# Probabilities-times-values products of a local attention, issued in halves with a 128-row product between the halves

## The reference, cut to what matters

```python
x = _layernorm(x + L0_attn(x))     # linear attention
x = _layernorm(x + L0_xattn(x))    # 4 experts
x = _layernorm(x + L0_ffn(x))      # 8 gated experts, golden weights
x = _layernorm(x + L1_attn(x))     # local attention in groups of 32 tokens
x = _layernorm(x + L1_xattn(x))    # attention over ctx
x = _layernorm(x + L1_ffn(x))      # shared and routed experts, top 2
```

```python
scores = jnp.einsum('bhgqd,bhgkd->bhgqk', qg, kg) / np.sqrt(hd)
attn = jax.nn.softmax(jnp.where(causal, NEG, scores), axis=-1)
out = jnp.einsum('bhgqk,bhgkd->bhgqd', attn, vg)
```

## Time and profile before

| | |
|---|---|
| time, median of 3 runs | 430.19 us (429.94 to 431.14) |
| span of the profiled execution, first to last instruction | 429.5 us |
| TensorE, busy | 413.5 us (96%) |
| GpSimd, busy | 270.6 us (63%) |
| VectorE, busy | 255.2 us (59%) |
| ScalarE, busy | 241.6 us (56%) |
| mean granted TensorE clock | 0.997 |
| chain that ended last, PE's share | 75% |

### The profile page before, as it was taken

How to read it: one execution, slowest core, us unless ns; L and a number is a source line. 1 busy time by engine, 2 the same in 40 slices (tenths; PEclk the granted TensorE clock), 3 DMA queues, 4 the chain that set the end, 5 groups by cost and what they waited for, 6 DMA issues and landing times.

```text
span 429.5 us, 9350 instructions
## 1 busy us (share of the span) xinstructions
PE 413.5 (96%) x3645; PEld 361.4 (84%) x3645; DVE 255.2 (59%) x637; ACT 241.6 (56%) x423; POOL 270.6 (63%) x237
## 2 busy tenths in 40 slices
PE   8999999999999999899999999999699999999994
PEld 7888999988889888788888899798578989888983
DVE  4778657748536338966654588655455676343243
ACT  4848654764484775352734767573526757554543
POOL 1744454564798577674876548457647386877763
PEclk9999999999999999999999999999999999999998
DMA  8644000021233313042222103121523332565402
GB/s 256 195 149 145 3 2 0 2 76 50 73 91 123 103 53 124 24 127 96 79 86 76 38 0 111 51 88 63 167 74 96 118 103 78 151 165 151 141 33 98
DMA packets 19623, 39.29 MB, mean 91 GB/s; under 512 B 2763, under 2 KB 7371, under 8 KB 19580
## 3 DMA queue, kind: packets, MB, share of 16 engines
q1 hardware_dynamic: 19004, 38.17, 28.8%
q10 hardware_dynamic: 576, 0.53, 0.4%
HBM read 37.08 MB, written 1.08 MB: 89 GB/s over the span
## 4 chain that ended last, share of the span: by engine, by line
PE 75%; DVE 10%; issue 4%; ACT 4%; DMA 3%; SPq 2%; POOL 1%; POOLq 0%; DVEq 0%; ACTq 0%
PE bank L492 13%; PE bank L493 13%; PE bank L495 13%; PE bank L762 8%; PE bank L764 7%; PE bank L763 7%; PE bank L842 2%; DMA pk_raw<-w_attn_dram 2%; PE bank L781 2%; PE bank L830 1%; DVE q_buf L1584 1%; DMA brow<-cw_dram 1%; PE bank L515 1%; PE bank L812 1%; PE bank L813 1%
## 5 line engine op out<-in xcount | busy, mean ns | idle before, releaser
L1307 POOL TENSOR_TENSOR h_lo<-hraw,h_hi 128x512 fp32r<-128x512 f32 x76 | 98.1, 1294 | 77.3 <-ACT h_hi L1097 77.2
L492 PE MATMUL bank<-xT_hi,pk_hi 128*128 128x512 f32 x256 | 102.9, 402 | 1.1 <-DVE hraw L1625 1.1
L493 PE MATMUL bank<-xT_hi,pk_lo 128*128 128x512 f32 x256 | 101.0, 395 | 0.0
L1097 ACT ACTIVATE h_hi<-hraw 128x512 fp32r<-128x512 f32 x76 | 47.8, 629 | 72.3 <-DVE hraw L1625 70.3
L1625 DVE TENSOR_TENSOR hraw<-bank,sil 128x512 f32<-128x512 f32 x76 | 52.4, 689 | 54.6 <-ACT sil L1085 24.6
L495 PE MATMUL bank<-xT_lo,pk_hi 128*128 128x512 f32 x256 | 80.4, 395 | 0.0
L762 PE MATMUL bank<-pk_hi,h_hi 128*128 128x256 f32 x272 | 77.8, 286 | 0.2 <-issue 0.2
L764 PE MATMUL bank<-pk_hi,h_lo 128*128 128x256 f32 x272 | 76.9, 283 | 0.0
L763 PE MATMUL bank<-pk_lo,h_hi 128*128 128x256 f32 x272 | 76.8, 282 | 0.0
L1313 POOL TENSOR_TENSOR pk_lo<-pk_raw,pk_hi 128x512 fp32r<-128x512 f32 (+1 forms) x44 | 74.8, 1700 | 2.8 <-ACT pk_hi L1115 2.6
L492 PEld LDWEIGHTS bank<-xT_hi,pk_hi 128*128 128x128 f32 x256 | 48.2, 188 | 11.8 <-DVE hraw L1625 1.6
(11 more groups left out here) (256 smaller groups left out, 736.6 us busy)
## 6 DMA issues: line engine op xcount, KB each, us to landing
pk_raw<-pk_f_dram SPq DMA_DIRECT2D x28, 384.0 KB, 3.3
pk_raw<-pk_f_dram SPq DMA_DIRECT2D x16, 512.0 KB, 3.5
pk_raw<-pk_f_dram SPq DMA_DIRECT2D x16, 256.0 KB, 3.3
kv_buf<-pk_x_dram SPq DMA_DIRECT2D x4, 512.0 KB, 3.7
x_tok<-x_rows_dram SPq DMA_DIRECT2D x1, 1024.0 KB, 9.5
pk_raw<-pk_x_dram SPq DMA_DIRECT2D x4, 256.0 KB, 6.2
brow<-cw_dram SPq DMA_DIRECT2D x4, 256.0 KB, 3.4
cw_late<-cw_dram SPq DMA_DIRECT2D x4, 256.0 KB, 4.0
```

What stands on the lines that cost most here:

```text
L492: pe.matmul(o, w(kc)[0], x(kc)[0], start=kc == 0, stop=False)
L493: pe.matmul(o, w(kc)[1], x(kc)[0], start=False, stop=False)
L1097: A(h_hi[:, row, at * 512:(at + 1) * 512], hraw[:, s % 2, :], ACT.Copy).then_inc(sems["hid_hi"], 1)
L1307: pool.tensor_tensor(h_lo[:, row, q], hraw[:, s % 2, :], h_hi[:, row, q].bitcast(F32), ALU.subtract).then_inc(sems["hid_lo"], 1)
```

## The change

Each `a1_values(T)` becomes two calls of 32 program matmuls (64 MATMUL records and 64 weight loads each): heads 0 to 7 where the whole stood, and heads 8 to 15 in a new step one product later. `a0.40`, `a0.55`, `a0.41`, `a0.56` are the second halves of tiles 0, 1, 2 and 3, and `a1.40` to `a1.56` those of tiles 4 to 7. Only the second half tells DVE. First halves keep the waits; second halves have none. The lists of the other engines are as before.

```diff
-u38 g39 u39 d18 a0.10 g40 u40 a0.25 g41 u41 a0.11 d19 a0.26 g42 d20 u42 g43 u43 g44 e0.2 e1.2 u44 e0.3 e1.3 g45 u45
+u38 g39 u39 d18 a0.10 g40 a0.40 u40 a0.25 g41 a0.55 u41 a0.11 d19 a0.41 g42 a0.26 d20 a0.56 u42 g43 u43 g44 e0.2 e1.2
...
-            def a1_values(T):
-
-                for hd in range(HEADS):
+            def a1_values(T, part):
+
+                for hd in range(part * HEADS // 2, (part + 1) * HEADS // 2):
...
-                m.then_inc(sems["a1_o_ps"], 1)
+                if part:
+                    m.then_inc(sems["a1_o_ps"], 1)
...
+                elif i in (40, 55, 41, 56):
+                    a1_values(T0 + (40, 55, 41, 56).index(i), 1)
```

More of the change, by code:

```diff
@@ L139 @@
 g31 u31 d14 d15 g32 u32 g33 u33 g34 e0.12 e1.12 u34 g35 u35 a0.3 d16 a0.4 g36 u36 g37 a0.5 a0.6 u37 a0.7 g38 a0.8 d17
-u38 g39 u39 d18 a0.10 g40 u40 a0.25 g41 u41 a0.11 d19 a0.26 g42 d20 u42 g43 u43 g44 e0.2 e1.2 u44 e0.3 e1.3 g45 u45
[L141 to L145, removed]
+u38 g39 u39 d18 a0.10 g40 a0.40 u40 a0.25 g41 a0.55 u41 a0.11 d19 a0.41 g42 a0.26 d20 a0.56 u42 g43 u43 g44 e0.2 e1.2
+u44 e0.3 e1.3 g45 u45 g46 e0.4 e1.4 u46 e0.5 e1.5 d21 g47 u47 e0.7 e1.7 d22 a0.22 d23 g48 u48 g49 e2.12 e3.12 u49 g50
+a0.24 a1.3 a1.4 u50 d24 a1.5 a1.6 a1.7 g51 a1.8 u51 g52 u52 d25 d26 d27 a1.10 g53 a1.40 u53 a1.25 g54 a1.55 u54 a1.11
+g55 a1.41 u55 a1.26 d28 a1.56 d29 d30 d31 g56 u56 e2.2 e3.2 g57 e2.3 e3.3 u57 g58 u58 e2.4 e3.4 d32 d33 e2.5 e3.5 g59
+u59 g60 u60 d34 e2.7 e3.7 g61 u61 a1.22 d35 d36 g62 d37 u62 g63 a1.24 u63 g64 u64 g65 u65 d38 g66 d39 d40 d41 u66 g67
+u67 g68 u68 d42 g69 u69 g70 u70 g71 d43 d44 d45 u71 g72 d46 u72 g73 u73 g74 u74 g75 u75 d47 e48 e49 e50 f48 e51 f49
+f50 f51
 """.split()
@@ L926, in attention @@
                     pe.wait_ge(sems["a1_pT"], 2 * h + 1)
-                    a1_values(T0)
+                    a1_values(T0, 0)
                 elif i == 25:
-                    a1_values(T0 + 1)
+                    a1_values(T0 + 1, 0)
                 elif i == 11:
@@ L932, in attention @@
                     pe.wait_ge(sems["a1_o"], T0 + 1)
-                    a1_values(T0 + 2)
+                    a1_values(T0 + 2, 0)
                 elif i == 26:
                     pe.wait_ge(sems["a1_o"], T0 + 2)
-                    a1_values(T0 + 3)
+                    a1_values(T0 + 3, 0)
+                elif i in (40, 55, 41, 56):
+                    a1_values(T0 + (40, 55, 41, 56).index(i), 1)
                 elif i == 22:
```

## The result

| | before | after |
|---|---|---|
| time, median of 6 runs each on one chip | 430.12 us (429.55 to 431.14) | 433.26 us (432.63 to 434.49) |
| ratio after to before, 95% interval | | 1.006 (1.0039 to 1.0081) |
| span of the profiled execution | 429.5 us | 431.3 us |
| TensorE, busy | 413.5 us | 415.5 us |

The change is slower by 0.6%. Before's span plus the same 1.8 is 431.3, some 1.1 us above its median.

What follows compares the result with a forecast made beforehand. TensorE, busy 413.5 of 429.5 us, was taken to bound the kernel, idling at instruction-block ends. First half +2.4 us and second half 0, on the 430.19 median, gave 432.6, rounded to 432.5 us; range 430.1 to 434.2.

Steps and rivals of the forecast that it cites:

- The price of going in and out: On PE, each of eight more runs of small products costs 0.30 us, 2.4 us in all, 1.2 per half of the batch.
- Tile 3 and `e1.2`: Tile 3 ends later; its chain of 8.3 us against PE's 6.3 makes PE wait 2.0 us at e1.2's transposes.
- The sum of the first half: Tiles 0 to 3: +1.2 for entries, -0.8 for holes removed, +2.0 wait at e1.2, together +2.4 us.
- Tile 4's block is late "because of a transfer that began before the tile": Tile 4's instruction fetch waits for a weights' transfer, block there at 305.93 again; PE waits 1.05 us instead of 2.7.
- Tile 5's block "comes at 311.67 again": Tile 5's fetch falls into the weights' transfer of 306.0 to 309.3 as before; PE waits 1.35 us.
- second half: 0: Tiles 4 to 7: what splitting gains is given back at e3.2, whose chain PE waits for; 0 us net.
- Rival 1: The fetches of tiles 4 and 5 clear, tile 5 ends 1.3 to 2.3 us earlier: 430.2 to 431.2 us; chance 0.20.
- Faster: All 5.6 us of idle time go and neither chain makes PE wait: 427.0 us; chance 0.12.
- The holes stay: PE's holes at small products remain; entries, e1.2 and e3.2 cost 3.8 us: 434.0 us; chance 0.15.
- same: Whole-kernel time within 0.3% (1.3 us) of before, 428.9 to 431.5 us; chance 0.20.
- rival 3: PE's holes at small products stay, with 3.8 us added: 434.0 us; chance 0.15.

Runs made afterwards that it cites:

- Experiment 2: The change with tile 3 whole in its old place: 430.1 us, ratio 0.9994; with tile 3's halves one product earlier: 430.57 us, 1.001.
- experiment 1: Against the kernel before: only tiles 0 to 3 split, 434.51 us, ratio 1.0078; only tiles 4 to 7 split, 429.94 us, 0.9983; before run again, 431.66 us.
- experiment 4: The kernel before, with one weights' transfer on SP held until tile 4 has ended: 431.09 us, ratio 1.001.
- experiment 5: The kernel before, with tile 3's first 10, 2 or 64 products issued twice: 426.22, 430.45 and 435.4 us, ratios 0.9924, 1.0013 and 1.0131.
- the weights held back: The kernel before, with one weights' transfer on SP issued only when tile 4 is done: 431.09 us, ratio 1.001.
- 2 and 64 products twice: The kernel before, with the first 2, or all 64, products of tile 3 issued twice: 430.45 us (ratio 1.0013) and 435.4 us (1.0131).
- the second half alone: The kernel before with only tiles 4 to 7 in halves, tiles 0 to 3 whole: 429.94 us, ratio 0.9983.
- the shift of 10: Tile 3's first 10 products issued twice: on the kernel before 426.22 us, ratio 0.9924; with tiles 4 to 7 also split 428.26 us, 0.9989.

## Why the prediction was right, and where two of its steps were not

The number (432.5 forecast, 433.26 measured), the sign and the mechanism that carries it held. That the number came so near is in part luck: the first half cost 1.0 us more than forecast, the second gave 0.7 that was not, and part of what was said of tiles 4 and 5 had the wrong cause.

*The price of going in and out* is right: 0.10 us beside 64 x 0.0085 at a half, 0.11 at the next step (231.79 to 232.13, where it is 0.23), and 0.09 more from the last product ahead of a half to its first record, 0.30 as forecast.

*Tile 3 and `e1.2`* is right. From tile 3's end to the issue of R1 pass 0.87 us (231.79 to 232.66; forecast 0.88) and from there to the end of the norm 7.39 us (to 238.96 + 1.09; forecast 7.40). The wait is 1.62 us in the list and 1.8 between starts. The product behind the transposes comes 2.8 us after their first one (237.49 to 240.30) where it took 0.8 in before (236.07 to 236.86): 2.0, as forecast. Experiment 2 shows that the place of tile 3 carries the sign, with down 20's wait, which goes with it.

*The sum of the first half* was too small: +2.4 forecast, +3.2 in the profiles and +3.4 in experiment 1. What was left out is the wait of down 20, 0.7 us. The prediction followed the delay of tile 3 through DVE and said nothing of tile 2, though its own rule was that DVE hears of a tile only after the second half; behind `a1_out` of tile 2 stand the additions that down 20 waits for.

*Tile 4's block is late "because of a transfer that began before the tile"* is wrong (experiment 4). Its packet starts late also with idle DMA engines; that PE's sequencer, standing at tile 4's wait, asks for it late is my reading (experiment 5). The time at which it is there counts from tile 4's start, so the forecast came out near for another reason: PE goes on 3.76 us after that start in before, 3.38 in after, 3.21 with the weights held back, 3.48 and 3.54 with 2 and 64 products twice. The forecast hole of 1.05 us was 0.7 in after and 0.6 with the second half alone.

*Tile 5's block "comes at 311.67 again"* is wrong as well. Its packet started in after while the weights were moving, and PE went on 5.2 us after it had gone on in tile 4, not 5.7: a hole of 0.8 between starts, not 1.35. With that tile 5 ended 0.9 us sooner, seen from tile 4's start (8.9 us against 9.7). The chain through R2, C7 to C9 and R3 to `e3.2` followed it, and took 0.8 us less itself between tile 5's end and the product behind `brow` (314.68 to 322.40, 7.7 us, against 8.5), and 0.2 less from there (DVE's timeline of after):

```profile
322.40 0.69 DVE L1613 TENSOR_TENSOR sil<-bank,brow 128x512 f32<-128x512 f32 x1 [2.13 <-DMA brow<-cw_dram]
```

So the term "second half: 0", from the step that the gain of tiles 4 to 7 is given back at `e3.2`, was mis-sized: -1.9 in this pair of executions, -0.7 over the runs of experiment 1. Rival 1 came true here in part.

*Faster* did not come, for the reason that was given: the chain from tile 3's end is 8.3 us long where 6.3 would have had to do. *The holes stay* did not come: 4.6 us became 1.1.

*Signs and chances.* Two of the signs missed. The idle time behind the small products was to fall to 2 to 3 us and fell to 1.1, and the wait at `e3.2` was to grow above 1 us and came to 0.52. The chances don't add up either: rival 1's 430.2 to 431.2 lies wholly inside "same", and forecast, rival 3 and half of rival 1 would be 0.75, not 0.68. Between the holes of tiles 4 and 5 the trace has 256 records, as the prediction says, but one of them only waits and one is the next weight load, not two that wait.

The Trainium skill, "Runtime: NRT & Kernel Launch", section on instruction fetch mechanics, calls the cost of a crossing mostly hidden. For the large products that agrees with the traces of before and after, since 29 packets left holes only at small products. With the second half split and the shift of 10, one crossing in down 28 cost 0.5 us, and a block that lies wholly in small products cost 2.4 us (experiment 5).

**What stays open:** the lengths of the holes vary between executions of one kernel by up to 1.6 us, which I can follow only in part (below); why the chain between tile 5 and `brow` was 0.8 us shorter in after; and what exactly makes PE ask for its next block.

## What to carry to other kernels

Before splitting or moving work, follow each end of it that another engine hears of, not only the last one: here two tiles were late, and both came back to PE. Where "issue" idles amid many small instructions at fixed places in the stream, look at the instruction queue. Here it was the place of the block's start that mattered, and a wait on a semaphore just behind it went with a late fetch. Moving the stream by 40 instructions gained more (0.76%) than any splitting (0.35%), with no dependence touched. Such a gain hangs on the instruction count of everything ahead, so it has to be looked at again after every edit. And before a gain is read from one pair of profiles, see how far each lies from its own median: 1.9 us of gain in the pair were 0.7 over the runs.

## What the runs showed of the hardware

After the hole of tile 4, in which PE stands for 2 us and more, TensorE's clock fell in four of six profiled executions. Busy time by stretch of the kernel before, run again (the column with 0.50 is PE's clock):

```profile
306.00:308.00 2.00, 1.87 (x8) 1.57 (x9) 0.68 (x2) 0.49 (x1) 2.00 (x3) 0.71 0.86 246
308.00:310.00 2.00, 2.00 (x6) 1.54 (x6) 0.00 (x0) 0.58 (x1) 2.00 (x3) 0.50 0.89 247
```

```profile
306.30 0.50 PE L492 MATMUL bank<-xT_hi,pk_hi 128*128 128x512 f32 x1
...
310.84 1.26 PE L842 MATMUL bank<-kv_buf,pT 32*32 32x17 f32 x128
```

Its products of 512 columns there are 0.43 us apart where they are 0.23 otherwise (307.28 to 307.71). At 0.50, which is 1.2 GHz of 2.4, gate 53 and up 53 took 4.5 us (306.30 to 310.84) where they took 3.0 (306.09 to 309.08), 1.6 us longer. Tile 5 then had no hole; that its block had that much more time is the likely reason. The first profiled execution kept its clock at 1.00 and had the hole of 1.6 us in tile 5 instead. With the weights held back the clock fell to 0.50 too (306 to 308), so tile 5's missing hole in that run doesn't show that the transfer had been its cause. So tile 4's hole costs about as much either way, 2.7 + 1.6 = 4.3 us with tile 5's hole or 2.4 + 1.6 = 4.0 with the fall of the clock. The shift of 10 products gained 3.3 us by its ratio (2.2 to 4.4). Shorter holes can do it too: with only tiles 4 and 5 in halves the clock was 0.50 from 316 to 318, after a hole of 1.4 us in tile 6. But the one of 2.5 us in tile 4 with 64 products twice left it at 1.00. I had not expected either.
